# Window attention in a fused transformer kernel: the value product with the exponentials as weights, its sums as columns, and the result turned by four products

## The reference

```python
xn = layer_norm(x) * g1 + b1                       # 48 channels
q, k, v = split(windows(xn) @ Wqkv + bqkv)         # 6 heads of 8, N = 49 tokens a window
attn = softmax(q @ k.T * 8 ** -0.5 + bias[head] + mask)
x = x + windows_back(attn @ v @ Wproj + bproj)
x = x + gelu((layer_norm(x) * g2 + b2) @ W1 + b1) @ W2 + b2   # 192 hidden
```

## Time and profile before

| what | value |
|---|---|
| median of three runs (lowest to highest) | 7914.44 us (7903.05 to 7923.93) |
| the profiled execution | 7950.78 us, span 7949.1 us |
| mean granted TensorE clock in it | 0.947 of full |
| share of the span busy | TensorE 94%, loads 67%, VectorE 47%, ScalarE 51%, GpSimd 28% |
| one turn at the full clock | 17.9 us |

### The profile page before, as it was taken

The page is one execution under the profiler, slowest core; times in us unless marked ns, Lnnn a source line. Parts: engine busy times, 40 slices in busy tenths (PEclk is TensorE's granted clock), DMA queues, the critical chain, the costliest instruction groups (busy, mean ns, idle before and its releaser), DMA issues.

```text
span 7949.1 us, 332425 instructions
## 1 busy us (share of the span) xinstructions
PE 7443.8 (94%) x144058; PEld 5332.6 (67%) x144058; DVE 3710.7 (47%) x7474; ACT 4083.7 (51%) x6145; POOL 2232.5 (28%) x2070
## 2 busy tenths in 40 slices
PE   6879999999999999999999999999999999999997
PEld 4856666666666676666666666676666666666664
DVE  5154444444444444444444444444444444444443
ACT  0035555555555555555555555555555555555551
POOL 3023223223232332322222222233223223222320
PEclk9999999999999999999999999999999999999995
DMA  7000000000000000000000000000000000000007
GB/s 228 1 18 21 22 20 21 22 21 22 20 22 20 22 22 21 22 20 20 20 22 20 20 22 21 20 22 23 20 22 22 19 22 22 19 22 20 22 18 213
DMA packets 287397, 242.85 MB, mean 31 GB/s; under 512 B 42174, under 2 KB 281760, under 8 KB 285856
## 3 DMA queue, kind: packets, MB, share of 16 engines
q1 hardware_dynamic: 241506, 179.61, 8.4%
q10 hardware_dynamic: 36414, 19.95, 0.8%
q0 software_dynamic: 8192, 22.49, 0.8%
HBM read 112.73 MB, written 109.18 MB: 28 GB/s over the span
## 4 chain that ended last, share of the span: by engine, by line
PE 84%; DVE 8%; issue 5%; DMA 3%; ACT 0%; SPq 0%; POOL 0%; POOLq 0%; DVEq 0%; ACTq 0%
PE pA L969 15%; PE pS L927 11%; PE pS L940 7%; PE pA L890 6%; PE pB L1026 5%; DVE V L716 4%; PE pA L1018 4%; PE pB L1009 4%; PE pB L1047 4%; PE pS L949 4%; PE pB L1066 4%; PE pA L896 3%; PE pB L978 3%; PE pA L986 3%; PE pA L1057 2%
## 5 line engine op out<-in xcount | busy, mean ns | idle before, releaser
L438 POOL TENSOR_TENSOR Kbd<-KT,headmask 128x588 f32<-128x588 f32 x768 | 895.4, 1166 | 3735.3 <-DVE KT L702 3735.3
L691 DVE TENSOR_REDUCE mx<-pS 113x12 f32<-113x588 f32 x1536 | 1180.4, 769 | 1162.2 <-PE pS L949 1146.7
L927 PE MATMUL pS<-bias,stackr 128*128 128x296 f32 x6096 | 1385.7, 351 | 3.5 <-ACT E L498 3.3
L482 ACT ACTIVATE sq<-pB 112x392 f32<-112x392 f32 x768 | 379.4, 494 | 1949.9 <-PE pB L978 1949.9
L498 ACT ACTIVATE E<-pS 113x588 f32<-113x588 f32 x1536 | 1006.7, 655 | 650.6 <-DVE mx L691 622.1
L438 POOL TENSOR_TENSOR Qbd<-Qt,headmask 128x588 f32<-128x588 f32 x768 | 895.9, 1166 | 1479.8 <-DVE Qt L696 1479.8
L969 PEld LDWEIGHTS pA<-E,V 113*64 113x64 f32 x36864 | 1149.8, 142 | 115.1 <-issue 114.9
L927 PEld LDWEIGHTS pS<-bias,stackr 128*128 128x128 f32 x6096 | 973.2, 197 | 342.7 <-issue 206.2
L969 PE MATMUL pA<-E,V 113*64 113x49 f32 x36864 | 1198.8, 227 | 0.8 <-ACT va L487 0.8
L940 PE MATMUL pS<-Kbd,Qt 24*49 24x147 f32 x24576 | 784.3, 311 | 0.0
L949 PE MATMUL pS<-Qbd,KT 27*49 27x147 f32 x24576 | 724.3, 291 | 0.0
(11 more groups left out here) (126 smaller groups left out, 10061.5 us busy)
## 6 DMA issues: line engine op xcount, KB each, us to landing
xin<-xT SPq DMA_DIRECT2D x384, 98.0 KB, 2.0
xT<-xout SPq DMA_DIRECT2D x384, 98.0 KB, 1.9
xin<-xT SPq DMA_DIRECT2D x384, 73.5 KB, 1.9
xT<-xout SPq DMA_DIRECT2D x384, 73.5 KB, 1.8
xT<-cm POOLq DMA_DIRECT2D x128, 171.5 KB, 3.6
cm<-xT SPq DMA_DIRECT2D x128, 171.5 KB, 3.4
tm<-in_x SPq DMA_DIRECT2D x128, 147.0 KB
out<-tm ACTq DMA_DIRECT2D x128, 147.0 KB
```

Of the source, the lines that this page charges most:

```text
L438: return pool.tensor_tensor(y, x, m, ALU.mult)
L691: dve.tensor_reduce(m, s, AX.X, ALU.max).then_inc(mx_done, 1)
L927: mm(pS[:, q, S1:S1 + 2 * SW], stackr[:, :], rows, start=True, stop=False)
```

## The change

The operands of the value product change places. `E` becomes the weights, in slices of 64 columns of which 49 are wanted, and `V3` streams: 18 columns, which are 8 values and a one for each of the two images. There are 48 products as before, each now complete in itself (no sum over three heads), alternately to partitions 0 to 63 and 64 to 127. The result has queries on partitions and heads along the free dimension, with the sums as every ninth column, in one bank of `pA`. VectorE takes the maximum of the 48 sums and 0.5 (for padding), makes reciprocals, and multiplies (`normalize`, tiles `den`, `rec`, `oN`), each waiting for the one before. TensorE turns `oN` back to channels on partitions by four products with the constant `select` (`turn`), and ScalarE copies the result to `oT` (`evac_o`). The copy to `oS`, the product with `spread`, the two activations of `inverse_sums` and GpSimd's multiply are gone. `up_c` now waits for `oN_done`. The projection's weights stand in plain order of channels, which makes for some fewer small loads in the set-up; `E` and `oN` are cleared once, and `V3` is smaller.

The core of the diff:

```diff
+        E = sb("E", [M2, 2, J * 4 * WN + HI - N])
+        den = sb("den", [M2, J * 2 * HEADS])
+        rec = sb("rec", [M2, J * 2 * HEADS])
+        oN = sb("oN", [M2, J, 2, HI])
+        oT = sb("oT", [R, 2, J, N])
         x1 = sb("x1", [R, 2, WIN, W])
         sq2 = sb("sq2", [R, 2, HT])
         va2 = sb("va2", [R, 2, HT])
@@ -195,6 +194,7 @@
 
 
         zeroed = sem("zeroed")
+        lined = sem("lined")
         const_in = sem("const_in")
         par_in = sem("par_in")
...
         s1_mm, mx_done, mxt_mm, qm_done = sem("s1_mm"), sem("mx_done"), sem("mxt_mm"), sem("qm_done")
         s2_mm, exp_done, pv_mm = sem("s2_mm"), sem("exp_done"), sem("pv_mm")
-        oS_done, sums_mm, lo_done, rb_done, oT_done = (
-            sem(n) for n in ("oS_done", "sums_mm", "lo_done", "rb_done", "oT_done"))
+        den_done, rec_done, oN_done, turn_mm, oT_done = (
+            sem(n) for n in ("den_done", "rec_done", "oN_done", "turn_mm", "oT_done"))
         proj_mm, x1_done, ctr2_mm, sq2_done, var2_mm, va2_done, rs2_done, xn2_done = (
             sem(n) for n in ("proj_mm", "x1_done", "ctr2_mm", "sq2_done", "var2_mm", "va2_done",
                              "rs2_done", "xn2_done"))
...
                 by_head(Qbd[:, j.mod(2)], Qt[:, j.mod(4)], half).then_inc(qbd_done, 1)
 
-            def normalize(j):
-                pool.wait_ge(rb_done, gv(j, 1, 1))
-                if not j.before(1):
-                    pool.wait_ge(proj_mm, gv(j, 1, 0))
-                pool.tensor_tensor(flat(oT), flat(oS), rb[:, :], ALU.mult).then_inc(oT_done, 1)
-
             def iteration(a, b, c, d, e, f):
-                if e:
-                    normalize(e)
                 if c:
                     spread_q(c, 0)
                 if b:
...
@@ -493,17 +484,17 @@
                 act.wait_ge(s2_mm, gv(j, 4, k + 1))
                 if b:
                     act.wait_ge(mx_done, gv(b, 4, k + 1))
-                e = strided(E[:, j.mod(2), k, 0, 0, 0:1], [[WN, 4], [1, WN]])
+                e = strided(E[:, j.mod(2), 4 * WN * k:4 * WN * k + 1], [[WN, 4], [1, WN]])
                 s = strided(pS[0:M2, 0, S2:S2 + 1], [[512, 4], [1, WN]])
                 act.activation(e, s, ACT.Exp).then_inc(exp_done, 1)
...
-            def inverse_sums(j):
-                act.wait_ge(sums_mm, gv(j, 1, 1))
-                act.activation(lo[:, :], pA[:, 1, 0:TOK], ACT.Ln).then_inc(lo_done, 1)
-                act.wait_ge(lo_done, gv(j, 1, 1))
+            def evac_o(j):
+                act.wait_ge(turn_mm, gv(j, 1, 1))
                 if not j.before(1):
-                    act.wait_ge(oT_done, gv(j, 1, 0))
-                act.activation(rb[:, :], lo[:, :], ACT.Exp, scale=-1.0).then_inc(rb_done, 1)
+                    act.wait_ge(proj_mm, gv(j, 1, 0))
+                src = strided(pA[0:R, 1, 0:1], [[2 * N, J], [N, 2], [1, N]])
+                dst = strided(oT[:, 0, 0, 0:1], [[N, J], [J * N, 2], [1, N]])
+                act.activation(dst, src, ACT.Copy).then_inc(oT_done, 1)
...
+            act.wait_ge(lined, 1)
...
+            chain(dve.memset(flat(E), 0.0))
+            chain(dve.memset(flat(oN), 0.0))
             chain(dve.memset(flat(V3), 0.0))
-            for h in range(HP):
-                for i in range(2):
-                    r, o = HI * i, 32 * i + HC + h
-                    last = dve.memset(strided(V3[r:r + N, 0, 0, h, o:o + 1], [[HP * HI, 4 * 2 * P]]), 1.0)
-            chain(last)
+            for i in range(2):
+                r, o = HI * i, (D + 1) * i + D
+                last = dve.memset(strided(V3[r:r + N, 0, 0, o:o + 1], [[2 * (D + 1), 4 * P * HEADS]]), 1.0)
+            last.then_inc(lined, 1)
...
-                    src = strided(pA[r:r + N, 0, 0:1], [[HC, 2 * P], [D, HP], [1, D]])
-                    dst = strided(V3[r:r + N, j.mod(4), 0, 0, 32 * i:32 * i + 1], [[HP * HI, 2 * P], [HI + D, HP], [1, D]])
+                    o = (D + 1) * i
+                    src = strided(pA[r:r + N, 0, 0:1], [[D, P * HEADS], [1, D]])
+                    dst = strided(V3[r:r + N, j.mod(4), 0, o:o + 1], [[2 * (D + 1), P * HEADS], [1, D]])
                     last = dve.tensor_copy(dst, src)
                 last.then_inc(v_done, 1)
 
-            def evac_o(j):
+            def normalize(j):
                 dve.wait_ge(pv_mm, gv(j, 1, 1))
+                e = D + 1
+                dve.tensor_scalar(den[:, :], strided(pA[0:M2, 0, D:D + 1], [[e, J * 2 * HEADS]]), 0.5, None, ALU.max)\
+                   .then_inc(den_done, 1)
+                dve.wait_ge(den_done, gv(j, 1, 1))
+                dve.reciprocal(rec[:, :], den[:, :]).then_inc(rec_done, 1)
+                dve.wait_ge(rec_done, gv(j, 1, 1))
                 if not j.before(1):
-                    dve.wait_ge(oT_done, gv(j, 1, 0))
-                dve.tensor_copy(oS[:, :, :], pA[0:RQ, :, 0:HT]).then_inc(oS_done, 1)
+                    dve.wait_ge(turn_mm, gv(j, 1, 0))
+                dve.tensor_tensor(strided(oN[:, 0, 0, 0:1], [[HI, 2 * J], [D, HEADS], [1, D]]),
+                                  strided(pA[0:M2, 0, 0:1], [[HEADS * e, 2 * J], [e, HEADS], [1, D]]),
+                                  strided(rec[:, 0:1], [[HEADS, 2 * J], [1, HEADS], [0, D]]), ALU.mult)\
+                   .then_inc(oN_done, 1)
...
-            def spread_sums(j):
-                pe.wait_ge(oS_done, gv(j, 1, 1))
-                mm(pA[:, 1, 0:TOK], spread[:, :], flat(oS), start=True, stop=True).then_inc(sums_mm, 1)
+            def turn(j):
+                pe.wait_ge(oN_done, gv(j, 1, 1))
+                for k in range(J):
+                    last = mm(pA[:, 1, 2 * N * k:2 * N * (k + 1)], oN[:, k].rearrange("p i c -> p (i c)"), select[:, :],
+                              start=True, stop=True)
+                last.then_inc(turn_mm, 1)
 
             def begin_scores(b, c, d, k):
 
@@ -962,13 +968,15 @@
             def values(j):
                 pe.wait_ge(exp_done, gv(j, 4, 4))
                 ready()
+                e = D + 1
                 for k in range(J):
-                    for wh in range(2):
-                        for h in range(HP):
-                            for hh in range(2):
-                                last = mm(pA[HI * hh:HI * hh + HI, wh, N * k:N * (k + 1)],
-                                          V3[:, j.mod(4), 2 * (J * wh + k) + hh, h, :],
-                                          E[:, j.mod(2), k, 2 * wh + hh, h, :], start=(h == 0), stop=(h == HP - 1))
+                    for h in range(HEADS):
+                        for wh in range(2):
+                            at, o = N * (HP * (4 * k + 2 * wh) + h), e * (2 * HEADS * k + h)
+                            last = mm(strided(pA[HI * wh:HI * wh + HI, 0, o:o + 1], [[HEADS * e, 2], [1, e]]),
+                                      E[:, j.mod(2), at:at + HI],
+                                      V3[:, j.mod(4), HEADS * (J * wh + k) + h, :].rearrange("p (i e) -> p i e", e=e),
+                                      start=True, stop=True)
                 last.then_inc(pv_mm, 1)
...
-                    pe.wait_ge(lo_done, gv(e, 1, 1))
+                    pe.wait_ge(oT_done, gv(e, 1, 1))
...
-                        pe.wait_ge(oS_done, gv(d, 1, 1))
+                        pe.wait_ge(oN_done, gv(d, 1, 1))
...
-                    spread_sums(d)
+                    turn(d)
...
```

More of the change, by code:

```diff
@@ L122, in build @@
         select = sb("select", [M2, 2 * N])
-        spread = sb("spread", [128, 128])
         wq = sb("wq", [R, NPH, HI])
@@ L238, in headcol @@
         def headcol(t, j, v, o=0):
-            heads = [q // 2 if j == BV else q % 2 for q in range(4)]
             return [(cols[32 * q:32 * q + HC, t, j:j + 1],
-                     v[o + HC * hh:o + HC * hh + HC].rearrange("(c a) -> c a", a=1)) for q, hh in enumerate(heads)]
+                     v[o + HC * (q % 2):o + HC * (q % 2) + HC].rearrange("(c a) -> c a", a=1)) for q in range(4)]
         par = []
@@ L1182, in constants @@
     minus = np.zeros((128, 1), np.float32)
-    spread = np.zeros((128, 128), np.float32)
     select = np.zeros((M2, 2 * N), np.float32)
@@ L1188, in constants @@
     for q in range(4):
-        spread[32 * q + HC, 32 * q + HC + HP:32 * q + 32] = 1.0
         for h in range(HP):
@@ L1193, in constants @@
             headmask[32 * q + HC + h, h] = 1.0
-            spread[32 * q + HC + h, 32 * q + D * h:32 * q + D * (h + 1)] = 1.0
-            spread[32 * q + HC + h, 32 * q + HC + h] = 1.0
     for r, m in ((0, 0), (HI, N)):
@@ L1207, in constants @@
     rel = ((i[:, None] - i[None, :] + WIN - 1) * (2 * WIN - 1) + j[:, None] - j[None, :] + WIN - 1)
-    return dict(ident=eye, center=center, ones=ones, headmask=headmask, minus=minus, stack=stack, select=select, spread=spread, kcol=kcol,
+    return dict(ident=eye, center=center, ones=ones, headmask=headmask, minus=minus, stack=stack, select=select, kcol=kcol,
                 regions=regions, rel_const=rel.reshape(-1).astype(np.int32))
```

27 lines of the change are left out of this document (11 added, 16 removed).

## The result

The changed kernel takes **9016.2 us** (median of 4 runs, 8993.4 to 9036.8) against 7908.7 us of the kernel before beside it: a ratio of 1.140 (95% interval 1.136 to 1.144). The profiled execution took 8993.42 us; that of before took 7950.78 us, so between the two profiles there are 1043 us to explain.

What follows compares the result with a forecast made beforehand. The prediction took TensorE's order through a turn, at one of two clock speeds, as the bound. 7951 us plus 296 direct plus 1017 for clock falls gave 9264, less 36: 9230 us, range 8180 to 10400 us.

Steps and rivals of the forecast that it cites:

- The value product keeps its pace: Value product: the load sets the pace, so it stays at 58 ns a pair, 3.0 us, despite the narrower stream.
- The normalization: Ahead of `up_c`: three VectorE instructions take 1.12 us in place of the copy's 0.57, 0.55 us a turn more, unhidden.
- The turn: `turn` on TensorE ahead of the fourth scores: 8 passes replace the product with `spread`, 0.22 us a turn more.
- The direct sum: Normalization and turning back together: 0.77 us a turn, times 384 = 296 us, between 130 and 580 us.
- The clock: End of the value product: short streams under long loads drop TensorE to 1.2 GHz; half of 339 turns, 6 us each, 1017 us.
- The ends of loop bodies: The 45 turns across the end of a body: left out of the turns that may fall, with no change forecast.
- The sum: Whole execution: 7951 + 296 + 1017 = 9264 us profiled, less 36 us for the median of runs: 9230 us.
- L859's stretch of short streams: Set-up: 49 columns loaded, 6 streamed, loads of 201 ns against 126; taken as 1.2 GHz for over 200 us though recorded busy.
- the clock holds: Rival for TensorE inside loop bodies: no falls, only the direct cost; 8210 us, 8050 to 8500 us, chance 0.22.

Runs made afterwards that it cites:

- experiment 2: Kernel before, with each value-product pass streaming 18 of the 49 query columns and the logarithm of the sums replaced by a constant; 8318.5 us, ratio 1.053.
- experiment 3: Changed kernel with value-product loads of 49 columns in place of 64; 8208 us, ratio 1.037.
- Experiment 5: Changed kernel with value-product streams of 54 columns and without `den` and `rec` (weights of `oN` a constant 1); 7850 us, ratio 0.993.
- experiment 6: Changed kernel with value-product streams of 54 columns and one product of 392 columns in place of the four of `turn`; 8116 us, ratio 1.027.
- experiment 1: Changed kernel with each value-product pass streaming 54 columns in place of 18, same loads and stand; 8120 us, ratio 1.027.
- experiment 9: Changed kernel with its 18 value-product columns repeated, streaming 54, 54, 36 or 18, output complete; 8190 us, ratio 1.035.
- experiment 7: Changed kernel with the third scores moved ahead of `up_c`, streams still 18 columns; 8586 us, ratio 1.086.
- experiment 11: Changed kernel with the value product in two halves around `up` and the third scores ahead of `up_c`; 8470 us, ratio 1.073.
- experiment 4: Changed kernel with the value product in two halves, `up` between them; 10352 us, ratio 1.310.

## Why the prediction was right

The forecast was 9230 us in a range of 8180 to 10400, and the time is 9016. By its steps:

- **The value product keeps its pace.** Right: 2.88 us of loads with 18, 49 and 54 columns streamed, and 2.28 us when 49 columns were loaded. Experiments 2 and 3 move the two sizes apart, so this is shown and not only argued.
- **The normalization, +0.55 us a turn.** Right in kind, and too small: the chain grew by 0.72 us. `den` took 0.21 us for 0.25, `oN` 0.56 as forecast; the reciprocal took 0.45 us, where 0.25 had been taken "as for its size". It was inside the bounds of 0.17 to 0.62. Experiment 5 shows that all of it is on the path.
- **The turn, +0.22 us.** Right: 0.24 us by experiment 6's full-clock turn.
- **The direct sum.** 296 us were forecast and 356 found, almost all of the difference being the reciprocal.
- **The clock, 1017 us.** The mechanism was right: low stretches begin behind the value product, inside loop bodies, and nearly all end ahead of the next one. The mean clock, 0.855, is in the 0.80 to 0.88 named, and turns come in kinds of 18.8 and 23 us and more. Of the 341 turns inside loop bodies 183 fell, 54% where half were taken. That share was a guess between none and all, as the prediction says, and that it came out so close is luck. The price was too high: 769 / 183 = 4.2 us a fall and not 6. This is the 4.2 us that had been worked out for a clock that rises again in the same turn, which nearly all did; next to no fall was of the kind for which 11 us had been worked out.
- **The ends of loop bodies.** The prediction left them as they were. They hold 338 us where they held 425, 87 us less, and why is open.
- **The sum.** Direct part +60 us, falls -248, ends -87: together -275, and the profiled execution came 271 us under the 9264 forecast for it. The median of the runs was put 36 us under that execution and lay 23 above it, and so the error of 9230 us is only 214. The errors offset each other in part.
- **Slips in the working.** Its own lower bound of 8500 us does not come out of its terms: 7951 + 130 + 0.1 x 339 x 6 - 36 gives some 8250 us. Its upper bound by the same terms is some 10530 and not 10400. L859's stretch of short streams in the set-up is not without a break: TensorE stands for 23.2 us up to 267.3 us. From there to 397.5 us its records have no gap of 0.5 us, and the reading of the loads stands on these 130 us.
- **The rival "the clock holds"**, 8210 us, is what wider streams give in the changed kernel (8120 and 8190 us in experiments 1 and 9); narrow ones don't. The Trainium skill (TensorE: Matmul & The Clock Gate, Part 1) tells of gaps in TensorE's work, and by gaps alone experiment 2 should have kept the clock of the kernel before. It had no added stand, and its waits at the loop ends sum to 181 us for 192 in the kernel before, yet its clock went from 0.947 to 0.897. The measurement decides: a record of TensorE as busy is not enough.

What is shown of the cause stands in this table, read from the profiled executions. A turn fell if a part of it was at 1.2 GHz; the microseconds are those over a full-clock turn of the same kernel (of experiment 11 for experiment 4, which has none).

| kernel | columns streamed | stand behind | turns fallen, of 341 | us in them | us at the 42 ends |
|---|---|---|---|---|---|
| before | 49 | none | 2 | about 0 | 425 |
| experiment 1 | 54 | 0.66 us | 3 | about 0 | 241 |
| experiment 9 | 54, 54, 36, 18 | 0.66 us | 13 | 4 | 318 |
| experiment 2 | 18 | none | 102 | 439 | 363 |
| changed | 18 | 0.66 us | 183 | 769 | 338 |
| experiment 7 | 18 | none | 118 | 559 | 249 |
| experiment 11 | 18, two halves | none | 28 | 42 | 478 |
| experiment 4 | 18, two halves | 1.48 us | 341 | 1845 | 564 |

Wide streams bring hardly a fall inside loop bodies, without the stand or with it. Narrow ones do without it, and more with it. What stays open is what the chip measures there, and what makes one turn fall and the next not, as 158 of them with the same instructions did not. The last column is not explained by any run.

## What to carry to other kernels

Where loads set the pace of a product, a narrower stream gains nothing at the full clock, and can cost TensorE its clock afterwards: ask of both orders of operands which has the longer stream for the same loads, and load no more columns than are wanted. Cost a change twice, by the turn at the full clock and by the number and length of low stretches; the mean clock tells the two apart before anything else is read. Ends of unrolled loop bodies cost a stand and a low stretch behind it, and twice the body gave here 3% for one number.

## What the runs showed of the hardware

- TensorE fell to 1.2 GHz while its records showed it busy: behind the 96 loads of 64 columns with 18 streamed, 2.98 us, it fell in 102 of 341 turns (experiment 2). In the changed kernel, streaming the same 18 columns three times in half of the products and twice in a quarter mended most of it (experiment 9, clock 0.956 for 0.855). Without a stand, the same products in two pieces of 1.58 us with 0.89 us of 392-column streams between them brought 28 falls (experiment 11).
- A stand of 0.66 us a turn cost no clock one stage behind wide streams (383 times in experiment 1), while one of 1.48 us directly behind narrow ones brought a fall in every turn (experiment 4, 10352 us). In the changed kernel the stand is 0.66 us and comes one stage behind the narrow streams, and some 54% of the turns fell. No run here parts the length of the stand from its place.
- A reciprocal on VectorE takes more than a tensor_scalar of the same tile: 113 x 48 in 0.45 us against 0.21 us.
- An end of a loop body of 8 turns cost about 425 / 42 = 10.1 us in the kernel before, of which (161.5 + 30.8) / 42 = 4.6 us are the stand of TensorE and the rest the low clock behind it. With 16 turns a body 224 us were gained. The stands without a shown releaser sum to 94 to 193 us in programs with 8 turns, and differ with edits that don't touch the loop's end.
